# The causal convolution of the first two half blocks moved from VectorE to TensorE, as products with diagonal matrices

## The reference

```
zxbcdt = layernorm(u) @ in_proj_kernel               # 256 -> z 512, xBC 768, dt 8
xp = pad(xBC, 3 zeros in front, along the sequence)  # per sequence
y  = conv1d_bias + sum over k of conv1d_weight[:, k] * xp[:, k:k+L]    # 4 taps, each channel by itself
xBC = silu(y)                                        # x 512, B 128, C 128 channels
dt = softplus(dt + dt_bias);  dA = -exp(A_log) * dt
Y  = chunked state-space scan over x, B, C, dA
u  = u + layernorm(rmsnorm(Y * silu(z)) @ out_proj_kernel)
out = u + layernorm(MLP(layernorm(u)))               # gate, up, down dequantized from 4-bit codes
```

## Time and profile before

| | before |
|---|---|
| median of 3 runs | 1014.07 us (1013.44 to 1014.91) |
| profiled execution | 1015.02 us, span 1013.3 us |
| PE busy | 922.1 us, 91% |
| DVE busy | 792.3 us, 78% |
| ACT busy | 599.6 us, 59% |
| POOL busy | 340.2 us, 34% |

### The profile page before, as it was taken

How to read it: one execution, slowest core, us unless ns; L and a number is a source line. 1 busy time by engine, 2 the same in 40 slices (tenths; PEclk the granted TensorE clock), 3 DMA queues, 4 the chain that set the end, 5 groups by cost and what they waited for, 6 DMA issues and landing times.

```text
span 1013.3 us, 17021 instructions
## 1 busy us (share of the span) xinstructions
PE 922.1 (91%) x6048; PEld 809.1 (80%) x6048; DVE 792.3 (78%) x2079; ACT 599.6 (59%) x1014; POOL 340.2 (34%) x346
## 2 busy tenths in 40 slices
PE   0546797999999999999999999999999999999987
PEld 0435696888988888878888888888888888888887
DVE  4989676888878987798878978798879988887132
ACT  4665949484646756484737656574737565682222
POOL 2013241524242423434242424334252424233232
PEclk9767898999999999999999999999999999999999
DMA  4212000000000000000000000000000000000000
GB/s 150 79 60 65 1 4 8 12 11 1 12 1 32 1 11 1 12 22 1 12 1 32 2 11 1 11 23 1 11 1 32 1 12 1 1 22 1 1 21 11
DMA packets 13828, 17.64 MB, mean 17 GB/s; under 512 B 1712, under 2 KB 10416, under 8 KB 13744
## 3 DMA queue, kind: packets, MB, share of 16 engines
q1 hardware_dynamic: 12880, 16.53, 5.1%
q10 hardware_dynamic: 864, 0.03, 0.1%
HBM read 12.36 MB, written 4.19 MB: 16 GB/s over the span
## 4 chain that ended last, share of the span: by engine, by line
PE 73%; DVE 14%; ACT 6%; issue 4%; DMA 1%; POOL 1%; ACTq 0%; DVEq 0%; POOLq 0%
PE fb L1088 28%; PE db L1088 14%; PE mb L1088 14%; DVE xc L892 6%; PE mb L1198 5%; PE mb L1189 3%; PE mb L1207 2%; PE mb L1181 2%; PE mb L1213 1%; ACT L704 1%; DVE stage L1051 1%; ACT lmat L637 1%; DMA dsk<-in_d_skip 1%; ACT xc L657 1%; DVE raw L883 1%
## 5 line engine op out<-in xcount | busy, mean ns | idle before, releaser
L554 POOL TENSOR_TENSOR hl<-hid,hl 128x512 fp32r<-128x512 f32 (+1 forms) x144 | 169.6, 1179 | 416.1 <-ACT hl L711 415.9
L1088 PE MATMUL fb<-x1t,wg 128*128 128x512 f32 (+1 forms) x864 | 214.5, 384 | 5.4 <-DVE x1t L994 5.3
L1088 PE MATMUL db<-wd,hl 128*128 128x256 f32 x1536 | 217.7, 290 | 1.6 <-POOL hl L554 1.5
L1088 PEld LDWEIGHTS db<-wd,hl 128*128 128x128 f32 x1536 | 198.7, 190 | 16.6 <-issue 9.6
L1088 PE MATMUL fb<-x1t,wu 128*128 128x512 f32 (+1 forms) x864 | 205.6, 374 | 3.5 <-ACT hid L704 3.5
L1088 PEld LDWEIGHTS fb<-x1t,wu 128*128 128x128 f32 x864 | 152.5, 191 | 37.2 <-ACT hid L704 6.5
L1088 PEld LDWEIGHTS fb<-x1t,wg 128*128 128x128 f32 x864 | 145.3, 191 | 30.5 <-DVE x1t L994 6.5
L1000 DVE TENSOR_TENSOR hid<-fb,hid 128x512 f32<-128x512 f32 (+1 forms) x144 | 90.2, 627 | 75.5 <-PE fb L1088 67.1
L711 ACT ACTIVATE hl<-hid 128x512 fp32r<-128x512 f32 (+1 forms) x144 | 83.4, 580 | 102.0 <-DVE hid L1000 75.4
L892 DVE SCALAR_TENSOR_TENSOR xc<-raw,cw,xc 128x256 f32<-128x256 f32 x288 | 132.9, 528 | 9.2 <-ACT xc L657 8.0
L704 ACT ACTIVATE hid<-fb 128x512 f32<-128x512 f32 (+1 forms) x144 | 78.3, 548 | 81.1 <-PE fb L1088 77.3
(11 more groups left out here) (140 smaller groups left out, 1382.7 us busy)
## 6 DMA issues: line engine op xcount, KB each, us to landing
xin<-in_u SPq DMA_DIRECT2D x16, 256.0 KB, 2.8
out<-xb SPq DMA_DIRECT2D x16, 256.0 KB, 2.2
words<-in_packed SPq DMA_DIRECT2D x12, 256.0 KB, 3.3
stage<-in_scales SPq DMA_DIRECT2D x12, 256.0 KB
wi_raw<-in_in_proj SPq DMA_DIRECT2D x2, 644.0 KB, 4.8
wo_raw<-in_out_proj SPq DMA_DIRECT2D x1, 512.0 KB, 10.8
cw<-in_conv_w ACTq DMA_DIRECT2D x1, 12.0 KB, 2.4
cb<-in_conv_b ACTq DMA_DIRECT2D x1, 3.0 KB, 2.8
```

The source lines that it names most:

```text
L554: pool.tensor_tensor(hl[:, hs, n % 2, 1, :], hid[:, hs, n % 2, :], hl[:, hs, n % 2, 0, :].bitcast(F32), ALU.subtract).then_inc(s["lo"], 1)
L1088: last = pe.matmul(ps, lhs(a, k), rhs(b, k), start=start and n == 0, stop=stop and n == len(todo) - 1, skip_group_check=check)
```

## The change

Where the half block is the second of block 0 or the first of block 1 (`CONV_ON_PE`), `conv` is a step of PE instead of DVE. DVE first builds, in one step `diags`, six tiles `diag` of 4 x 128 x 128: for every tap a diagonal matrix of the tap's weights. ACT's `taps` then only copies the projection to `raw`. PE's `conv` makes eight fp32 products of 256 columns, four taps for each of the two channel tiles, into the projection's own bank, and `silu` reads that bank, twice 256 columns, with the conv's bias as its own. So an `ip` bank stays taken until `silu`. The history copies become DVE steps `hist_in` and `hist_out`. The `diag` tiles lie where the last quarter of the weights `wg`, `wu`, `wd` will be, so that `dl:9`, `dl:10` and `dl:11` on both engines wait for the last `conv` of PE. All other half blocks are as before, and so are `ORDER` and `LAST`; `FIRST` is written in another order on all four engines.

```diff
-        seg:1> seg:2> gu:1 dn:0 gb:0> xtr:0> gu:2 gu:3 yo:0> seg:3> yd:0> st:0> dn:1 dn:2 yt:0> xtr:1> gu:4 dn:3
+        xt:0> st:2 yd:2 yt:2 xtr:3 out:2 yo:3 yd:3 st:3 yt:3 out:3 z:0> z:1> ip:0> ip:1> x1t:1 conv:0> conv:1>
+        z:2> ip:2> conv:2> gu:0 cs:0> ct:0> seg:0> seg:1> seg:2> dn:0 gu:1 gb:0> xtr:0> gu:2 gu:3 yo:0> seg:3>
...
+CONV_ON_PE = ((0, 1), (1, 0))
...
+        def conv_on_pe(i, k):
+            return (i + k // 3 // 2, k // 3 % 2) in CONV_ON_PE
...
+        def diag_read(eng, q):
+            if q >= MATS * (PIECES - 1):
+                i, j = CONV_ON_PE[-1]
+                eng.wait_ge(s["conv"], count("conv", i, 3 * j + 2))
...
                 ps = m_bank["ip", k][:].rearrange("p (two t) -> p two t", two=2)
+                if conv_on_pe(i, k - 2):
+                    act.wait_ge(s["conv"], count("conv", i, k - 2))
                 act.activation(raw[:, k % 2, :, TAPS - 1:], ps, ACT.Copy).then_inc(s["raw"], 1)
+                if conv_on_pe(i, k):
+                    return
...
+                if conv_on_pe(i, k):
+                    for e, name in enumerate(("tap", "xc")):
+                        ct = 2 * pr + e
+                        act.activation(xc[:, ct, :], m_bank["ip", k][:, SUB * e:SUB * e + SUB], ACT.Silu,
+                                       bias=cb[:, ct:ct + 1]).then_inc(s[name], 1)
+                    return
...
+            def diags(i, par, _):
+                dve.wait_ge(ident_ready, 1)
+                dve.wait_ge(small_loaded, 96)
+                for ct in range(CT):
+                    last = dve.tensor_tensor(diag[ct], ident[:].unsqueeze(1).broadcast_to([P, TAPS, P]),
+                                             cw[:, ct, :].unsqueeze(2).broadcast_to([P, TAPS, P]), ALU.mult)
+                last.then_inc(diag_ready, 1)
...
+            def conv(i, par, k):
+                if (i, k) == (0, 3):
+                    pe.wait_ge(diag_ready, 1)
+                pe.wait_ge(s["raw"], count("raw", i, k))
+                pe.wait_ge(s["hin"], count("hin", i, k))
+                for e in range(2):
+                    ct = 2 * (k % 3) + e
+                    for tap in range(TAPS):
+                        last = pe.matmul(m_bank["ip", k][:, SUB * e:SUB * e + SUB], diag[ct][:, tap, :],
+                                         raw[:, k % 2, e, tap:tap + SUB], start=tap == 0, stop=tap == TAPS - 1)
+                last.then_inc(s["conv"], 1)
```

More of the change, by code:

```diff
@@ L110 @@
-        xtr:2> gu:13 xt:0>> yd:2> st:2> dn:11 yt:2> gu:14 xtr:3> out:2> yo:3> yd:3> gu:15 x1t:0> dn:12 yt:3>
-        st:3> out:3> z:0>> z:1>> dn:13 dn:14 ip:0>> ip:1>> dn:15 x1t:1> ip:2>> z:2>>""",
-    "act": """
[L113 to L118, removed]
+        xt:1 ip:3 conv:3 z:3 ip:4 conv:4 z:4 ip:5 conv:5 cs:1 z:5 ct:1 seg:4 seg:5 seg:6 gb:1 seg:7 yo:2 xtr:2
@@ new lines @@
+        xtr:3> out:2> yo:3> dn:12 yd:3> gu:15 dn:13 yt:3> st:3> x1t:0> out:3> z:0>> z:1>> dn:14 ip:0>> ip:1>>
+        dn:15 x1t:1> ip:2>> z:2>>""",
+    "act": """
+        xn_split:1 wi_split:0 wi_z:0 dq:0 wo_split:0 dq:1 dl:0 dq:2 dl:1 dq:3 dl:2 taps:3 dq:4 dl:3 dq:5 taps:4
+        dl:4 silu:3 dq:6 gate:3 gate:4 rates:0 dt_bias:1 taps:5 dl:5 silu:4 gate:5 silu:5 exps:1 decay_sums:4
+        decay_matrix:4 decay_sums:5 decay_matrix:5 decay_sums:6 decay_matrix:6 decay_sums:7 decay_matrix:7
+        gb_copy:1 xn_split:0> dq:7 yt_split:2 square:2 dl:6 dq:8 dl:7 dq:9 dl:8 yt_split:3 square:3 gate:0>
+        taps:0> dt_bias:0> x1_split:1 taps:1> gate:1> dq:10 gate:2> silu:0> taps:2> dq:11 dl:9 dl:10 dl:11
+        silu:1> silu:2> gelu:0 split:0 decay_sums:0> exps:0> decay_matrix:0> decay_sums:1> decay_matrix:1>
@@ new lines @@
+        square:1> split:6 gelu:7 split:7 gelu:8 split:8 taps:3> gelu:9 gate:3> gate:4> taps:4> silu:3>
+        dt_bias:1> gelu:10 taps:5> split:9 split:10 gate:5> silu:4> silu:5> decay_sums:4> exps:1>
+        decay_matrix:4> decay_sums:5> decay_matrix:5> decay_sums:6> decay_matrix:6> decay_sums:7>
+        decay_matrix:7> gelu:11 gelu:12 split:11 gb_copy:1> xn_split:0>> split:12 gelu:13 square:2> yt_split:2>
+        split:13 gelu:14 gelu:15 split:14 yt_split:3> square:3> x1_split:0> dt_bias:0>> split:15 gate:0>>
@@ L142 @@
     "pool": """
         stats1:1 wi_split:0 stats1:0> xdt:2 yoff:2 xdt:3 yoff:3 stats2:2 ln2:2 stats2:3 ln2:3 split:0 split:1
[L144 to L146 removed]
+        xdt:0> split:2 yoff:0> split:3 stats1:1> xdt:1> split:4 yoff:1> split:5 stats2:0> ln2:0> split:6 split:7
@@ L147 @@
+        split:8 stats2:1> stats1:0>> split:9 split:10 xdt:2> yoff:2> split:11 split:12 ln2:1> split:13 xdt:3>
+        yoff:3> stats2:2> ln2:2> split:14 stats2:3> split:15 ln2:3> fin:0""",
 }
@@ L346, in build @@
         a_ready = sem("a_ready")
+        diag_ready = sem("diag_ready")
         wi_hi = sem("wi_hi")
```

93 lines of the change are left out of this document (59 added, 34 removed).

## The result

The changed kernel takes 1028.95 us (median of 4, 1027.88 to 1029.41) against 1013.76 for the kernel before beside it: 1.0141 times as long, 95% interval 1.0127 to 1.0156. It is slower, as forecast, but by about twice what was forecast (+14.3 by the ratio, +7.1 predicted), and lies 2 us above the range.

A forecast was written before the change was run, and what follows sets the result against it. It took DVE to bound the start, ACT 150 to 175 us and PE the time after 205 us. 2.0 (terms 1 to 3) + 9.0 - 3.9 made +7.1, so 1021 us, range 1005 to 1027.

The forecast's parts named there:

- term 4: Block 1's first half, `ip:0` to second gelu: PE convs in turns with ACT, three `dl` ahead of silus; +9.0 us.
- term 5: Block 1's second half: six table loads on ACT instead of nine; -3.9 us, bounds 0 and 6.
- term 3: From `xdt:2` to `ip:0` of block 1: weight work leaves DVE; -3.1 us, so +2.0 at `ip:0`.
- term 2: Block 0 up to `xdt:2`: ACT and PE take turns; +5.1 us in all, up to +8 at half clock.
- term 1: The start, at `xn_split:1`: diagonals and history copies on DVE; +1.3 us, or 0 if POOL does not hold DVE.
- Rival (c): Half clock too: +5 us left at `ip:0`, 10 in block 1's first half; +11, 1025 us; chance 0.16.
- Rival (a): DVE sets the start and is relieved of six convs: 999 us at best, or 1004 to 1005; chance 0.24.
- Rival (d): PE conv unnoticed at 0.95 us each: term 4 +1.5, term 2 about +3; 1012 to 1013; 0.18 shared with another rival.

The follow-up runs named there:

- pe_block1: Changed kernel with block 0's three convs back on DVE and the diagonals made behind `dl:5`; convs on PE in block 1 only: 1.0125 of before.
- order_only: Changed kernel's new order of all four lists, but all convs on DVE and no diagonals: 1.0113 of before.
- short_chain: Changed kernel with block 1's `ip:2` and `conv:2` ahead of `z:2` and the three `dl` behind `gelu:2`: 1.0230 of before.
- pe0_new_order: Kernel before with block 0's convs on PE, in lists there written around the wait for the bank: 1.0064 of before.
- order1_alone: Kernel before up to `xdt:2`, the changed kernel's lists from there on, convs on DVE, no diagonals: 1.0078 of before.
- tail_on_before: Kernel before with the changed kernel's lists from `gu:7` on (block 1's second half), nothing else: 0.9989 of before.

## Why the prediction came out as it did

The direction and the chain of term 4 were right. Two steps failed. In term 5, "Three loads are 3.85 us" priced three table loads as if all of ACT's time stood in the chain; they gave 1.5 us in the trace and 1.1 by the ratio. In term 3, the relief of DVE was followed through with the chain's products at the price of before; the chain moved from DVE to PE and gave 1.6 us instead of 3.1. Terms 2 and 4 were mis-sized by 1.6 and 1.9 us, and the causes that they name are not the only ones.

**The start (term 1, +1.3).** 0.17 at `xn_split:1`. The term had the diagonals begin when POOL's subtraction ends, at 14.2; they ran from 12.01 to 16.9, partly beside it, though at 4.89 us instead of 3.6 to 4 (3.69 in pe_block1, where POOL did nothing meanwhile). What the term did not see is that the new order by itself wins the start: with `rates:0` moved away and no diagonals, order_only has `xn_split:1` at 23.75 us. The diagonals took 4.7 us, and the moved `rates:0` had given 2.9 to 4.6 over the starts of before (26.7 to 28.3).

**Block 0 (term 2, +5.1).** 6.7 in the profile shown, 5.2 to 5.3 in three others with the same lists, 7.9 in short_chain. The forecast times hold within 1.2 us up to `conv:5`, which starts at 51.88 (52.4 forecast). The term took that conv at full clock, 3.4 us; it took 5.41, and 3.72 in the three others. With "up to +8" at half clock the term had named this. The cause that it names, ACT and PE in turns, is real (pe0_new_order), but the order without a conv on PE ends at the same mark (order_only). How much of the changed kernel's delay each has is not shown.

**To `ip:0` (term 3, -3.1).** Mis-sized: -1.6, in the changed kernel and in order1_alone alike. The step that failed is "whose products run partly at half clock as before". The granted clock over this leg is as before, 0.68 and 0.69, but the chain is another. In the kernel before it runs through DVE, with about 6 us of PE's products in it; in the changed kernel there are about 15, among them `z:0` and `z:1` at 2.49 us (1.90 before). With DVE relieved the leg is as long as the clock makes it: 34.4 us at 0.60, 32.3 to 32.9 at 0.68, 30.6 and 28.6 at 0.83 and 0.88. With the lists of before it is 34.2 to 35.3 at anything from 0.61 to 0.81.

**Block 1's first half (term 4, +9.0).** +10.9. The chain was forecast link for link and summed to 9.7, of which 9.0 were taken. But that the convs on PE with the bank are its cause is not borne out: with the convs on DVE the same order costs as much (order1_alone, 32.7 against 33.0). With the convs on PE a better order wins 4.5 us at this mark and loses 3.5 of them before `ip:3`; 5.4 stay. "What comes on top stands on ACT", the three `dl` at 3.15 us, is worth 1.1, since the pieces have to stand somewhere.

**Block 1's second half (term 5, -3.9).** The largest error for its size: -1.5 in the trace, -1.1 by tail_on_before. The three loads did go, but the term took ACT's time for the chain's. PE's product for `gelu:9`, 2.78 us late, was next at once, one of the bounds that the term had named (0).

**The sum.** The measured terms are 6.7 - 1.6 + 10.9 - 1.5 = +14.5, and +14.3 is the ratio. Of the 7.4 us missed, 1.6 are term 2, 1.5 term 3, 1.9 term 4 and 2.4 term 5, all on the same side, so the range (to 1027) was too narrow on it. Rival (c), 1025 us with the half clock too, was the nearest, and its case reached to 1029; but its reason holds only for block 0 and the way to `ip:0`, for block 1's first half had a clock of 0.90. Rival (a), DVE relieved, did not come: DVE had its time back and 1.6 us of it reached the chain. Rival (d), a cheap conv, is excluded by 3.72 us a conv; its sum takes +1 up to `ip:0`, where its own terms, +3 and -3.1, make -0.1.

## What to carry to other kernels

Before the cost of a moved operation is judged, run the new order with the old operation: here the order that came with the change cost 11 of 14 us by itself. That does not make the moved operation free: in lists written for it the convs on PE still cost 6 us in block 0. A chain names one path; another of the same length may stand beside it, and then undoing the change as named gives nothing. A tuned list pays for each step out of its place, mostly through what is queued behind it (`ip:2` behind `z:2` behind a gate: 4.4 us). And a saving on an engine is worth only what its next wait leaves: three table loads of 1.28 us gave 1.1 together.
